# A recommendation tower on one core: sample pairs side by side in the feature tile, one-hot rows of two tables per instruction, compact sums of the dense weights

## The reference

```
e = stack([tbl_i[ids[:, i]] for i in range(26)], axis=1)       # 512 x 26 x 128, fp32
c = concatenate([dense[:, None, :], e], axis=1)                # 512 x 27 x 128
g = einsum('bfd,bgd->bfg', c, c)                               # 27 x 27 products per sample
z = concatenate([dense, g[:, upper triangle without diagonal]])  # 128 + 351 columns
h = concatenate([z, dense])                                    # 607 columns
h = maximum(h @ W_top1 + b_top1, 0)                            # 512 columns
h = maximum(h @ W_top2 + b_top2, 0)                            # 256 columns
y = h @ W_top3                                                 # one number per sample
```

## Time and profile before

| | |
|---|---|
| device time, three runs | 112.77 us median (111.9 to 113.47) |
| span of the profiled execution, first to last instruction | 110.6 us |
| busy in the span | PE 98.0 us (89%), DVE 87.3 us (79%), ACT 85.4 us (77%), POOL 67.7 us (61%) |
| first stage, PE's first to last hot matmul | 7.9 to 60.1 us |
| TensorE clock granted | full speed throughout |

### The profile page before, as it was taken

How to read it: one execution, slowest core, us unless ns; L and a number is a source line. 1 busy time by engine, 2 the same in 40 slices (tenths; PEclk the granted TensorE clock), 3 DMA queues, 4 the chain that set the end, 5 groups by cost and what they waited for, 6 DMA issues and landing times. The chain is left out here.

```text
span 110.6 us, 2569 instructions
## 1 busy us (share of the span) xinstructions
PE 98.0 (89%) x931; PEld 77.7 (70%) x931; DVE 87.3 (79%) x216; ACT 85.4 (77%) x180; POOL 67.7 (61%) x68
## 2 busy tenths in 40 slices
PE   4967989949999999999999976999999977987991
PEld 2334846538788877768667965899899876975960
DVE  4469989689999999988989899945992849999001
ACT  4369697999999999999971899966796679683310
POOL 3577777777777777788888977777777700000000
PEclk9999999999999999999999999999999999999999
DMA  4889989944987789999110123212222210000000
GB/s 75 278 294 362 357 246 390 330 169 76 281 172 261 289 170 381 413 378 310 56 27 25 42 68 77 65 49 61 67 70 54 74 25 0 6 0 0 0 0 1
DMA packets 7868, 16.59 MB, mean 150 GB/s; under 512 B 2156, under 2 KB 3568, under 8 KB 7600
## 3 DMA queue, kind: packets, MB, share of 16 engines
q1 hardware_dynamic: 5648, 11.84, 31.9%
q0 software_dynamic: 1920, 3.94, 12.6%
q10 hardware_dynamic: 288, 0.66, 2.2%
HBM read 16.43 MB, written 0.00 MB: 148 GB/s over the span
## 5 line engine op out<-in xcount | busy, mean ns | idle before, releaser
L329 POOL DMA_INDIRECT rows<-in_gathered_tables,row_at x60 | 66.8, 1114 | 20.1 <-issue 17.7
L695 PE MATMUL gram_ps<-one_hot,table_hi 128*128 128x512 f32 x94 | 38.8, 413 | 4.3 <-DVE one_hot L512 2.5
L697 PE MATMUL gram_ps<-one_hot,table_lo 128*128 128x512 f32 x94 | 37.0, 394 | 0.0
L512 DVE TENSOR_SCALAR one_hot<-hot_ids_sb,row_ids 128x512 fp32r<-128x512 int32 x83 | 35.4, 480 | 1.9 <-DMA hot_ids_sb<-in_hot_ids 1.9
L540 DVE COPY pairs<-gram_ps 27x128 f32<-27x128 f32 (+3 forms) x76 | 25.3, 333 | 6.0 <-PE gram_ps L633 4.9
L695 PEld LDWEIGHTS gram_ps<-one_hot,table_hi 128*128 128x128 f32 x94 | 17.6, 188 | 13.3 <-DVE one_hot L512 5.4
L435 ACT COPY pairs<-gram_ps 27x128 f32<-27x128 f32 (+3 forms) x68 | 22.7, 334 | 3.9 <-PE gram_ps L633 3.1
L697 PEld LDWEIGHTS gram_ps<-one_hot,table_lo 128*128 128x128 f32 x94 | 17.7, 189 | 2.5
L633 PE MATMUL gram_ps<-features_t 128*59 128x56 f32 x512 | 15.9, 219 | 1.9 <-ACT features_t L344 1.3
L633 PEld LDWEIGHTS gram_ps<-features_t 128*59 128x59 f32 x512 | 14.7, 134 | 3.6 <-ACT features_t L344 1.7
L400 ACT COPY features_t<-gram_ps 128x512 f32<-128x512 f32 (+2 forms) x12 | 12.3, 1040 | 4.9 <-PE gram_ps L697 4.9
(11 more groups left out here) (45 smaller groups left out, 58.1 us busy)
## 6 DMA issues: line engine op xcount, KB each, us to landing
table_sb<-in_hot_tables SPq DMA_DIRECT2D x10, 512.0 KB, 5.6
hot_ids_sb<-in_hot_ids SPq DMA_DIRECT2D x11, 256.0 KB, 4.8
w_pairs_sb<-in_w_pairs SPq DMA_DIRECT2D x1, 1024.0 KB, 8.6
w_again_sb<-in_w_again SPq DMA_DIRECT2D x1, 1024.0 KB, 11.2
rows<-in_gathered_tables,row_at POOLq DMA_INDIRECT x60, 4.9
table_sb<-in_hot_tables ACTq DMA_DIRECT2D x1, 512.0 KB, 5.2
w_sb<-in_w SPq DMA_DIRECT2D x1, 512.0 KB
table_sb<-in_hot_tables SPq DMA_DIRECT2D x2, 128.0 KB, 5.3
```

The source lines that it names most:

```text
L329: pool.indirect_dma_start(rows[:, p % rows_ring, m, :], None, gathered_tables, bass.IndirectOffsetOnAxis(ap=row_at[:, t, at:at + 1], axis= ...
L512: nc.vector.tensor_scalar(one_hot_at(i), hot_ids_sb[:, of % ids_ring, :], row_id(n, c), None, ALU.is_equal).then_inc(one_hot_dve, 1)
L695: nc.tensor.matmul(hot_bank(of), table_hi[:, n % 3, own], one_hot_at(i), start=(begins and c == 0), stop=False)
L697: last = nc.tensor.matmul(hot_bank(of), table_lo[:, n % 3, own], one_hot_at(i), start=False, stop=(ends and c == count - 1))
```

## The change

It does three things.

**Layout.** `features_t` becomes 256 pairs of samples x 32 slots x 2, with the two samples of a pair adjacent. A hot table's copy now writes two neighbours and then jumps 64 elements; a transposed pass is read from PSUM in runs of two and written in runs of 24 (or 6). The samples are permuted on the host so that a copy of `pair_block` writes 16 samples in a row; its source elements stay 64 apart. The products read their operands with a step of 2 elements and take 64 and 54 columns in place of 59 and 56.

**Hot tables in groups.** The eleven tables form six groups, the first of one table and the others of two. DVE makes the one-hot rows of both tables of a group in one instruction of 1024 columns; ACT makes none. The tables are split in pieces of at most four parts (512 columns), 25 in all, each rounded and copied by ACT (`split_piece`) and subtracted by DVE (`low_part`). PE uses one-hot tiles from a ring of eight parts.

**Weights and zeros.** The two dense weight blocks come as compact rows, are added by one DVE instruction in the last group, and go to their places in `w_pairs_sb` by 14 DMAs from SBUF to SBUF, issued on SP ahead of `join_dense`. `layer1` waits for them (`w_joined`). POOL zeroes half of the spare slots and half of `pairs` ahead of its gathers; DVE's two larger memsets of `pairs` go. Two of the four warm-up matmuls go.

```
-STEPS = ((0, 8, 2), (0, 0, 8), (1, 8, 2), (1, 0, 8), (2, 8, 2), (2, 0, 8)) + tuple((n, 0, 8) for n in range(3, len(HOT)))
-STEP_PARTS = 8
+HOT_GROUPS = ((0,), (2, 3), (1, 7), (13, 16), (19, 21), (23, 25))
+GROUP_PARTS = (10, 10, 8, 8, 8, 8)
...
-TURN_EARLY = {5 + p: p for p in range(9)}
...
-WARM = (4, 4, 4, 2)
+TURN_BEHIND = {(1, 9): 0, (2, 3): 1, (2, 7): 2, (3, 3): 3, (3, 7): 4, (4, 3): 5, (4, 7): 6, (5, 3): 7, (5, 7): 8}
+
+WARM = (4, 4)
...
+def sample_order():
+
+    return [first + (2 * h + a) * (size // 4) + q for first, size in PIECES for q in range(size // 4) for a in range(2) for h in range(2)]
...
-    table_ring, ids_ring, rows_ring = 5, 5, 9
+    piece_ring, ids_ring, rows_ring, hot_ring = 8, 3, 9, 8
...
-        features_t = sbuf("features_t", [P, batch, SLOTS])
+
+        features_t = sbuf("features_t", [P, batch // 2, SLOTS, 2])
...
-            b, nq = first % P + j, size // 4
-            at = 2 * COLUMNS * (j % 2)
-            src = gram_ps[32 * j:32 * j + FEATURES, n % 2, 0:nq, at:at + 2 * COLUMNS].rearrange("p q (h c) -> p q h c", h=2)
-            src = src[:, :, :, k:k + 4 * (count - 1) + 1:4].rearrange("p q h i -> p h i q")
-            return pairs[32 * k:32 * k + FEATURES, first // P % 2, :, 0:count, b:b + 4 * (nq - 1) + 1:4], src
+            nq = size // 4
+            b = first % P + nq * j
+            at = FEATURES * (j % 2)
+            src = gram_ps[32 * j:32 * j + FEATURES, n % 2, 0:nq, at:at + 2 * COLUMNS].rearrange("p q (h c) -> p h c q", h=2)
+            return pairs[32 * k:32 * k + FEATURES, first // P % 2, :, 0:count, b:b + nq], src[:, :, k:k + 4 * (count - 1) + 1:4, :]
...
-                sp.dma_start(w_again_sb[:, :, :], w_again).then_inc(pair_weights_in, 16)
...
+                sp.wait_ge(w_summed, 1)
+                sp.wait_ge(pair_weights_in, 16)
+                for d, (p, i) in enumerate(dense_places()[:dim]):
+                    if d == 0 or dense_places()[d - 1] != (p - 1, i):
+                        run = 1
+                        while d + run < dim and dense_places()[d + run] == (p + run, i):
+                            run += 1
+                        sp.dma_start(w_pairs_sb[p:p + run, i, :], w_dense_sb[d:d + run, 0, :]).then_inc(w_joined, 16)
+                sp.wait_ge(pairs_zeroed, 1)
                 join_dense(0)
                 join_dense(1)
...
+                nc.gpsimd.memset(features_t[:, batch // 4:, FEATURES:SLOTS, :], 0.0).then_inc(slots_zeroed, 1)
+                nc.gpsimd.memset(pairs[:, :, 1, :, :], 0.0).then_inc(pairs_zeroed, 1)
...
+                for q in pieces_of(0):
+                    split_piece(q)
+                for g in range(n_groups):
+                    if g >= 1:
+                        place_hot(g - 1)
+                    ahead = pieces_of(g + 1) if g + 1 < n_groups else []
+                    turns = [p for (tg, c), p in sorted(TURN_BEHIND.items()) if tg == g]
+                    for q in ahead[:2]:
+                        split_piece(q)
+                    for p in turns[:-1]:
+                        place_pass(p)
+                    for q in ahead[2:]:
+                        split_piece(q)
+                    if g == n_groups - 1:
+                        place_hot(g)
+                    for p in turns[-1:]:
+                        place_pass(p)
...
+                for g in range(n_groups):
+                    for c in range(GROUP_PARTS[g]):
+                        one_hot_part(g, c)
...
+                        if 1 <= g < n_groups - 1:
+                            behind = (5, 6, 8, 9) if g == 1 else (1, 3, 5, 7)
+                            if c in behind:
+                                low_part(pieces_of(g + 1)[behind.index(c)])
+                        if g == n_groups - 1 and c == 3:
+                            sum_dense_weights()
...
-                for n in range(PAIR_PARTS):
-                    nc.vector.tensor_tensor(w_pairs_sb[:, n, :], w_pairs_sb[:, n, :], w_again_sb[:, n, :], ALU.add).then_inc(w_summed, 1)
...
-                            b = first + q * 4 + 2 * h
-                            last = nc.tensor.matmul(gram_ps[64 * h:64 * h + SLOTS + FEATURES, n % 2, q, 0:4 * COLUMNS],
-                                                    flat_features[:, b * SLOTS:b * SLOTS + SLOTS + FEATURES],
-                                                    features_t[:, b:b + 2, 0:2 * COLUMNS], start=True, stop=True)
+                            two = first // 2 + 2 * q
+                            last = nc.tensor.matmul(gram_ps[64 * h:64 * h + 2 * SLOTS, n % 2, q, 0:2 * FEATURES],
+                                                    features_t[:, two:two + 2, :, h].rearrange("p a s -> p (a s)"),
+                                                    features_t[:, two:two + 2, 0:FEATURES, h], start=True, stop=True)
```

More of the change, by code:

```diff
@@ L58, in pair_places @@
                     yield 32 * k + g, i, None, False
-FREE_ROWS = ((27, 5, 0, 4), (59, 5, 0, 4), (91, 5, 0, 3), (123, 3, 0, 3), (64, 64, 3, 1))
+FREE_ROWS = ((27, 5, 0, 4), (59, 5, 0, 4), (91, 5, 0, 3), (64, 64, 3, 1), (123, 5, 0, 3))
 def dense_places():
-    return [(p, i) for row, rows, part, parts in FREE_ROWS for p in range(row, row + rows) for i in range(part, part + parts)]
+    return [(p, i) for row, rows, part, parts in FREE_ROWS for i in range(part, part + parts) for p in range(row, row + rows)]
 def pieces():
@@ new lines, in row_id, with tables_through, hot_table, parts_through @@
+        def row_id(g, c):
+            return row_ids[:, int(GROUP_PARTS[g] != GROUP_PARTS[-1]), c:c + 1]
+        def tables_through(g):
+            return sum(len(group) for group in HOT_GROUPS[:g + 1])
+        def hot_table(g, t):
+            return tables_through(g) - len(HOT_GROUPS[g]) + t
+        def parts_through(g, c):
+            return PARTS.index((g, c)) + 1
+        def piece_uses(q):
+            g, t, first, count = PIECES_HOT[q]
+            return parts_through(g, first + count - 1)
@@ new lines, in pieces_of, with piece_columns, piece_with @@
+        def pieces_of(g):
+            return [q for q, piece in enumerate(PIECES_HOT) if piece[0] == g]
+        def piece_columns(of, q, c=None):
+            g, t, first, count = PIECES_HOT[q]
+            span = slice(0, count * dim) if c is None else slice((c - first) * dim, (c - first + 1) * dim)
+            return of[:, q % piece_ring, span]
+        def piece_with(g, t, c):
+            return [q for q, (pg, pt, first, count) in enumerate(PIECES_HOT) if (pg, pt) == (g, t) and first <= c < first + count][0]
@@ new lines, in place_hot @@
+                def place_hot(g):
+                    act.wait_ge(part_used, parts_through(g, GROUP_PARTS[g] - 1))
+                    for first, end in ((0, BLOCK), (BLOCK, batch)) if g == n_groups - 1 else ((0, batch),):
+                        for t in range(len(HOT_GROUPS[g])):
+                            act.copy(features_t[:, first // 2:end // 2, 1 + hot_table(g, t), :],
+                                     hot_bank(g, t)[:, first:end].rearrange("p (b two) -> p b two", two=2)).then_inc(hot_placed, 1)
@@ L450, in _ @@
                 act.wait_ge(weights_in, 16 * n_other_loads)
+                act.wait_ge(pairs_zeroed, 1)
                 pairs_of_act(0)
```

400 lines of the change are left out of this document (163 added, 237 removed).

## The result

The changed kernel takes 125.14 us in the median of four runs (123.5 to 126.1), the kernel before 112.87. The ratio is 1.106, with a 95% interval of 1.095 to 1.116. The profiled run took 126.08 us with a span of 124.2; before, the span was 110.6. So 13.6 us are to be found in the two traces, of which the medians have 12.3.

A forecast was written before the change was run, and what follows sets the result against it. ACT was taken to set the first stage's pace, with DVE and PE close behind. Start 0, loop +9.3, pair copies -2.1 and SP +0.3 sum to +7.5 us: 120.3 us, range 116.5 to 125.3.

The forecast's parts named there:

- the loop: First stage, groups 2 to 4: ACT, DVE and PE wait in turn, 12.2 us per two tables against 8.8; +9.3 us.
- full wait on SP: Upper end of the range: the second stage waiting fully on SP's queue adds up to 4.7 us.
- slow copies: Upper end of the range: rivals 1 to 3, copies or placed passes staying or becoming slow, 122.4 to 123.7 us.
- The start: First stage, groups 0 and 1: PE's last matmul of the third table at about 25 as before; 0, -0.5 to +1.
- The clock: Fewer warm-up matmuls: granted clock might fall ahead of the first products, slowing group 0's parts; 0, at most +1.
- Pair copies: Second stage: 128 elements in 0.28 in place of 0.388 us; -2.1 us, between 0 and -4.
- rival 1: Pair copies: source elements 256 bytes apart keep each copy at 0.39, so no gain; 122.4 us, 15%.
- SP: Second stage: weight moves and `join_dense(0)` issues on SP's queue land just in time for the first fold; +0.3, 0 to +5.
- Products: Second stage: 54 columns for 56, weights 64 for 59, read with a step of two; taken as 0.
- rival 4: Products: PE reads features with a step at half rate, up to +14 us, 134 us; 5%.
- Rivals 2 and 3: Placed passes become slow, 123.7 us, 12%; copies of finished tables do not get cheaper, 122.6 us, 5%.
- Rival 5: First stage: ACT, relieved of work, stays ahead and PE runs through groups 2 to 5; 107.2 us, 3%.

The follow-up runs named there:

- the undisturbed pair: few_before and few_after, the kernel before and the changed kernel with nine of 60 gathers: 112.1 and 123.6 us.
- few_two_ahead: Changed kernel with ACT's order rewritten to prepare pieces for the group after next, and nine of 60 gathers: 108.0 us, ratio 0.963.
- few_after: Changed kernel with the gathers of three passes only, nine of 60: 123.6 us, ratio 1.102.
- filler: Changed kernel with idle matmuls for PE in the stalls of groups 2, 3 and 4: 153.8 us beside 139.9 of the kernel before, ratio 1.105.
- few_before: Kernel before with the gathers of three passes only, nine of 60: 112.1 us beside 112.2 with all gathers, ratio 0.998.
- pool_pause_2: Changed kernel, POOL issuing gathers of passes 14 and up only after the first two pieces of products: 162.7 us beside 138.5 of the kernel before.
- few_layout: Kernel before with the new layout alone and nine of 60 gathers: 108.0 us, ratio 0.960.
- the third series: Series of the four kernels with nine of 60 gathers, on a chip where the kernel before with all gathers took 112.2 us.

## Why the prediction was right, and where its sizes were off

The forecast was 120.3, range 116.5 to 125.3; measured 125.14. The sign and the mechanism, the loop, held. That the number lies inside the range is partly luck. The change cost 12.3 us where 7.5 were forecast, and what filled the gap, the half clock and the late first pair copy, is not what the range had kept room for (a full wait on SP, slow copies). The full wait on SP puts the upper end at 120.3 + 4.7 = 125.0 and not at 125.3, and the measurement lies between the two. By its own steps:

- **The start, 0.** Right, if half a microsecond better. The last matmul of the third table starts at 24.42 in place of 25.03, and in the undisturbed pair at 24.52 and 24.54.
- **The loop, 12.2 us for groups 2 to 4.** Right where the clock stayed full: 12.31 and 12.26 us in group 3, 7.99 for group 5 where 7.8 was said. The stalls of 2.7 and 1.65 measured 2.34 and 1.37 there. That few_two_ahead has none of it shows the order of ACT as the cause (its edit also puts the first two pieces of group 2 ahead of everything on ACT that waits for PE's groups, as working two groups ahead needs).
- **The clock, "0, at most +1".** This is the term that was mis-sized. I looked for a fall at the start, in group 0, not behind the stalls that I had just forecast. The fall in group 0 came too (the granted clock was 0.50 from 9 to 12 us) and cost nothing at the end of the third table. Groups 2 and 4 took 14.07 and 13.70 against 12.31 for the same work: 3.2 us in the profiled run, the slowest of the four. PE's granted clock fell to half (1.2 GHz of 2.4) behind stalls of 2.3 us, though not behind every one: in few_after it did so in group 4 alone, for 1.4 us. With fillers group 4 took 1.5 us less than without.
- **Pair copies, 0.28 for 128 elements.** Measured 0.289 on DVE and 0.256 on ACT: right in price, and rival 1 is refuted. The yield was 1.4 at the opening (1.6 said) and 0.4 for the rest (0.5 said).
- **SP, +0.3.** Right by errors that cancel. The 14 moves held the queue for 0.70 each and not 0.40, 4.3 us more in all. But the five issues of `join_dense(0)`, priced at 3.9 from the kernel before, took 2.3. The change also regroups these rows (`(i r) b -> r i b` for `(r i) b -> r i b`), which neither the list of changes nor the forecast has. First the moves of the changed kernel, then the issues of few_after, beside the earlier trace rows:

```profile
67.26 9.85 SPq L337 DMA_DIRECT2D w_pairs_sb<-w_dense_sb  x14
...
L325 SPq DMA_DIRECT2D pairs<-in_dense_t x20: 258/307/566, 75.7 to 96.1; - x20
```

  In few_after the rows also landed 1.0 sooner behind the issues than forecast, and the pair copies were done 2.2 later (78.9 for 76.7). The fold waited 0.43 in few_after and not at all in the changed kernel; the moves landed long before layer 1 at 83.9.
- **Products, 0.** Mis-sized: the new form cost 1.3 to 1.5 us of busy time (17.1 or 17.3 against 15.8). It has 64 weight columns for 59, 54 moving ones for 56 and a step of two, and no run separates these. The first pair copy of few_after comes 0.44 later behind the last hot matmul than that of few_before; 0.2 of this is the products, the rest the three more transposes that stand ahead of them. A read with a step of two is not half rate; rival 4 is refuted.
- **What no term had:** the first pair copy was 2.5 us later than this in the profiled run (5.84 against 3.29 in few_after). Some 0.5 of it are gaps between products. The other 2.0 lie between the end of the sixty-fourth product and its signal, which the trace has at 78.20; in the four traces with nine gathers every signal of PE stands within 0.03 us of the end of its matmul. pool_pause_2 shows, on a disturbed chip, that both kinds of delay are gone while POOL is idle; few_after agrees, but it also ran on another chip. How the gathers delay PE or its signals stays open.
- **Rivals 2 and 3** are refuted by 491 and 630 ns. Rival 5, ACT staying ahead, is refuted by the loop itself. The one-hot of 1024 columns took 744 to 760 ns; I took 0.81, and the 0.75 that I estimated from the Trainium skill's page "VectorE: DVE Perf Modes", section "The perf-mode tier table", was the better value.

In the undisturbed pair the parts are: loop +11.3 (1.4 of it clock), first products +0.44, pair copies -1.4 and -0.4, SP +0.43, together 10.4, the difference of the two spans (120.6 and 110.2). The loop cost more than the whole change; its layout alone is worth -4.1 us there (few_layout against few_before), and brought no gain on the disturbed chips.

## What to carry to other kernels

Taking work off the engine that sets the pace is worth nothing if the new order makes that engine start its next step from the end of the current one: walk once round the loop of handovers before counting busy time. Work for the group after next, placed where the engine would otherwise wait, took 15.6 us off with not one instruction fewer, in the kernels with nine gathers. Where a stall of PE is forecast, price the clock behind it as well, from rows at half clock.

## What the runs showed of the hardware

- With two neighbours of 4 bytes at the target, a copy of 512 elements from PSUM fell from 1121 ns (one element, then a jump of 128 bytes) to 630; a wholly contiguous one took 602. The pair copies, with a source in PSUM 256 bytes apart and the target in a row, took 289 ns for 128 elements on DVE and 256 on ACT; the forecast's estimate without any cost of the source was 280.
- A short DMA of five rows of 2 KB from SBUF to SBUF held SP's queue for 0.70 us, as long as the nested loads of the kernel before (0.72 in the median). The same loads with their rows regrouped at the source took 0.31.
- On some chips PE stands still, for 12 us and more in all, while POOL issues gathers, and the copy that waits for one of its signals starts 14.6 us behind the recorded end of the transposes (`filler`). It did so between 20 and 52 us and again in the first products, and ran at full pace beside gathers in between. On the chip of the third series the 60 gathers cost the kernel before nothing (112.2 against 112.1 us with nine).
